# A two-layer cross-attention kernel on one core: the two layers as two phases, and MLP products from rounded halves

## What is computed

```python
# layer 0
h = ln(x, ln1);  q, k, v = h @ sa_wq, h @ sa_wk, h @ sa_wv
x = x + attn(rope(q * scale), rope(k), v, causal=True) @ sa_wo
h = ln(x, ln2);  q = h @ ca_wq;  k, v = y @ ca_wk, y @ ca_wv
x = x + attn(rope(q * scale), rope(k), v, causal=False) @ ca_wo
h = ln(x, ln3);  x = x + gelu_tanh(h @ fc1) @ fc2
# layer 1
q = x @ Wq.T;  k, v = y @ Wk.T, y @ Wv.T
x = x + attn(q * scale, k, v, causal=True)
x = ln(x);     out = x + gelu(x @ W1.T) @ W2.T
```

## Time and profile before

| | |
|---|---|
| median of 3 runs | 1119.66 us (1118.54 to 1122.07) |
| span of the profiled execution | 1118.3 us |
| own time of the profiled execution | not given beside its span; the span is 1.4 us under the median |
| PE busy | 936.4 us, 84% |
| DVE busy | 582.5 us, 52% |
| ACT busy | 419.9 us, 38% |
| POOL busy | 73.3 us, 7% |
| mean granted PE clock | 0.930 |

### The profile page before, as it was taken

The page is one execution under the profiler, slowest core; times in us unless marked ns, Lnnn a source line. Parts: engine busy times, 40 slices in busy tenths (PEclk is TensorE's granted clock), DMA queues, the critical chain, the costliest instruction groups (busy, mean ns, idle before and its releaser), DMA issues.

```text
span 1118.3 us, 13782 instructions
## 1 busy us (share of the span) xinstructions
PE 936.4 (84%) x5180; PEld 456.9 (41%) x5180; DVE 582.5 (52%) x1347; ACT 419.9 (38%) x822; POOL 73.3 (7%) x83
## 2 busy tenths in 40 slices
PE   3888864899988898888989867999887888987898
PEld 1433322345443353434445324633233454442365
DVE  5555637784667704488545675665125504415500
ACT  1133331342355625353422431167763323343421
POOL 2102000000000200000000001000000000000210
PEclk9988886799999999988999897999998999998999
DMA  7805462202132100645020401013004004022000
GB/s 275 102 1 73 75 139 43 24 2 27 23 38 30 29 1 20 94 51 66 1 30 1 57 13 17 10 40 48 1 20 57 2 1 57 2 37 22 1 19 19
DMA packets 47013, 43.85 MB, mean 39 GB/s; under 512 B 13510, under 2 KB 44386, under 8 KB 46434
## 3 DMA queue, kind: packets, MB, share of 16 engines
q1 hardware_dynamic: 46948, 42.98, 24.0%
HBM read 13.32 MB, written 2.10 MB: 14 GB/s over the span
## 4 chain that ended last, share of the span: by engine, by line
PE 57%; DVE 17%; DMA 10%; ACT 8%; SPq 5%; issue 4%; ACTq 0%; DVEq 0%
PE ps_exp L852 10%; PE ps_o L964 10%; PE ps_misc L835 10%; PE ps_max L889 8%; ACT probs L1200 5%; DVE mcol L1114 5%; SPq L695 4%; PE ps_exp L922 4%; DMA QA<-part 4%; PE ps_chain L814 3%; PE ps_chain L822 3%; DVE swap L1028 2%; DMA QC<-part 2%; PE ps_exp L927 2%; PE ps_chain L787 2%
## 5 line engine op out<-in xcount | busy, mean ns | idle before, releaser
L1114 DVE TENSOR_REDUCE mcol<-ps_max 128x3 f32<-128x462 f32 (+5 forms) x496 | 292.2, 626 | 181.9 <-PE ps_max L891 106.1
L1200 ACT ACTIVATE probs<-ps_exp 128x512 f32<-128x512 f32 (+3 forms) x544 | 261.1, 523 | 242.0 <-PE ps_exp L925 87.0
L889 PE MATMUL ps_max<-KA,QA 96*128 96x512 bf16 (+3 forms) x384 | 117.9, 359 | 55.3 <-DVE mcol L1114 24.4
L922 PE MATMUL ps_exp<-QA,KA 98*128 98x512 bf16 (+3 forms) x384 | 120.4, 350 | 26.1 <-ACT probs L1200 18.3
L835 PE MATMUL ps_misc<-hT,w_up 128*128 128x512 f32 x256 | 125.7, 615 | 7.2 <-ACT hid L1191 2.2
L852 PE MATMUL ps_exp<-w_down,hid 128*128 128x256 f32 x512 | 128.2, 388 | 0.0
L1191 ACT ACTIVATE hid<-ps_misc,col 128x512 f32<-128x512 f32 x64 | 44.0, 687 | 200.4 <-PE ps_misc L835 200.4
L852 PEld LDWEIGHTS ps_exp<-w_down,hid 128*128 128x128 f32 x512 | 94.5, 190 | 29.7 <-issue 15.5
L1248 POOL TENSOR_TENSOR part<-rot,part 128x512 bf16<-128x512 f32 (+1 forms) x36 | 40.8, 1133 | 923.2 <-DVE part L1038 923.2
L889 PEld LDWEIGHTS ps_max<-KA,QA 96*128 96x128 bf16 x384 | 39.2, 104 | 123.1 <-DVE mcol L1114 63.6
L964 PE MATMUL ps_o<-probs,V 128*17 128x512 f32 (+3 forms) x768 | 85.1, 517 | 3.2 <-ACT probs L1200 2.3
(11 more groups left out here) (109 smaller groups left out, 986.6 us busy)
## 6 DMA issues: line engine op xcount, KB each, us to landing
QA<-part SPq DMA_DIRECT2D x72, 128.0 KB, 5.1
QC<-part SPq DMA_DIRECT2D x72, 128.0 KB, 5.2
KA<-part SPq DMA_DIRECT2D x48, 128.0 KB, 5.2
xb<-in_x SPq DMA_DIRECT2D x8, 512.0 KB, 6.1
out<-xb SPq DMA_DIRECT2D x4, 512.0 KB, 3.0
KC<-part SPq DMA_DIRECT2D x24, 77.0 KB, 3.1
w_up<-in_fc SPq DMA_DIRECT2D x1, 1024.0 KB, 7.0
w_down<-in_fc SPq DMA_DIRECT2D x1, 1024.0 KB, 8.2
```

Of the source, the lines that this page charges most:

```text
L889: mm = pe.matmul(dst, q, kk, start=True, stop=not causal)
L922: mm = pe.matmul(bank[:, q0:CH], KA[:, g // NT, hh, (g % NT) * P:(g % NT + 1) * P], QA[:, hh, q0:CH], start=True, stop=(r < 0))
L1114: dve.tensor_reduce(dst, src, AX.X, ALU.max).then_inc(s_max_done, 1)
L1200: act.activation(probs[:, n % 2, h, q0:CH], ps_exp[exp_nth[s] % 2][:, q0:CH], ACT.Exp).then_inc(s_exp_done, 1)
```

## The change

1. **Two phases.** `post(c)` is cut into `layer0(c)` and `layer1(c)`. The thread of slot 0 now runs layer0 of chunks 0, 1 and 2 and then layer1 of chunks 2, 0 and 1. The x of chunks 0 and 1 goes to HBM after layer 0 (`save`) and comes back before layer 1 (`load3`), which waits until the chunk before it has been stored. A new step `phase2`, after the last `pv` of all self-attention, loads what layer 1 wants into the place of KA, V and the self-attention weights: w_up1, w_down1, KC1, l1_wq and the norm's rows. No step of layer 1 can come before it.
2. **MLP products.** Weights and activations are held as a high half (rounded to float32r) and a low half (the rest, also float32r). Each product is three float32r matmuls, high x high, high x low and low x high: `up` has 6 matmuls of 512 columns, `down` has 12 of 256. The input halves are made by two more ACT evictions and one POOL subtraction per `tr` of ln3 and ln4; the hidden halves by a second gelu on ACT and a POOL subtraction per `up`.
3. **Weights split at the start.** ACT loads the four weight matrices one by one to a staging place (`wload`), ACT rounds, POOL subtracts (`wsplit`), and layer 1's halves are written to HBM (`wsave`) ahead of layer 0's split. Layer 1's context keys go to HBM too (`keepkc`). `late` is gone.
4. **Context tail.** The four copies of the tail tokens are laid out as 128 columns in the input, so that one group of matmuls takes the place of four.
5. **Small moves.** `lnout` goes from POOL (8 operations) to DVE (2). The splitting of the bias rows goes from DVE to POOL, where it stands first. The planner's prices change with it.

```diff
-def post(c):
-    return (post_norm("sa", "ln2", c) + cross("ca", c) + out_norm("ca", "ln3", c)
-            + mlp(0, c) + [("tr", "x3", c, g) for g in range(NT // 2)] + cross("la", c)
+def layer0(c):
+
+    return post_norm("sa", "ln2", c) + cross("ca", c) + out_norm("ca", "ln3", c) + mlp(0, c)
+
+
+def layer1(c):
+
+    return ([("tr", "x3", c, g) for g in range(NT // 2)] + cross("la", c)
             + [("addatt", c, g) for g in range(NT // 2)] + norm("ln4", c) + [("lnout", c)] + mlp(1, c)
             + [("store", c)])
...
+KEPT = (0, 1)
+BEHIND = (2, 0, 1)
...
+def post():
+
+    out = []
+    for c in range(LAST):
+        out += layer0(c) + [("save", c)] * (c in KEPT)
+    for c in BEHIND:
+        out += [("load3", c)] * (c in KEPT) + layer1(c)
+    return out
...
+HALVES = ((0, 0), (0, 1), (1, 0))
...
                     for t in range(KT):
-                        mm = pe.matmul(bank[:, :], w_up[l][:, t, m * P:(m + 1) * P], hT_of("up", c)[:, t, :],
-                                       start=(t == 0), stop=(t == KT - 1))
+                        for i, j in HALVES:
+                            mm = pe.matmul(bank[:, :], w_up[l][:, i, t, m * P:(m + 1) * P], hup[:, j, t, :],
+                                           start=(t == 0 and (i, j) == HALVES[0]),
+                                           stop=(t == KT - 1 and (i, j) == HALVES[-1]))
...
-                        mm = pe.matmul(dst, hid[:, m % 2, t * P:(t + 1) * P], w_down[l][:, m, :],
-                                       start=False, stop=(m == NM - 1), skip_group_check=True)
+                        for i, j in HALVES:
+                            mm = pe.matmul(dst, hid[:, n % 2, i, t * P:(t + 1) * P], w_down[l][:, j, m, :],
+                                           start=False, stop=(m == NM - 1 and (i, j) == HALVES[-1]),
+                                           skip_group_check=True)
...
+                    gelu = (ACT.Gelu_apprx_tanh, ACT.Gelu)[l]
+                    act.activation(gel[:, n % 2, :], ps_misc[:, :], gelu, bias=c0(("fc1_b", "l1_b1")[l], m))
+                    act.activation(hid[:, n % 2, 0, :], ps_misc[:, :], gelu,
                                    bias=c0(("fc1_b", "l1_b1")[l], m)).then_inc(s_misc_free, 1)
...
+                elif k == "up":
+                    n = up_nth[s]
+                    after_misc(pool, s)
+                    pool.tensor_tensor(hid[:, n % 2, 1, :], gel[:, n % 2, :], hid[:, n % 2, 0, :],
+                                       ALU.subtract).then_inc(s_hid, 1)
...
+                if k == "wsplit":
+                    _, i, j = s
+                    src, high, _ = weight_half(i, j)
+                    if j == 0:
+                        act.wait_ge(s_stage[i % 2], 16 * (i // 2 + 1))
+                        if i > 1:
+                            act.wait_ge(s_wsaved[i % 2], 16)
+                    act.activation(high, src, ACT.Copy).then_inc(s_high, 1)
...
+                elif k == "wsave":
+                    i = s[1]
+                    act.wait_ge(s_wsplit, 2 * (i + 1))
...
-                    for j in range(HG):
-                        dst = bank[32 * j:32 * j + LYB, E:2 * E]
-                        add_bias(dst, name, LYB, start=False)
-                        for t in range(KT):
-                            mm = pe.matmul(dst, cT[:, t, b * LY + P:(b + 1) * LY], w_ctx[:, 2 * l + 1, t, :],
-                                           start=False, stop=(t == KT - 1), skip_group_check=True)
+                    dst = bank[:, E:2 * E]
+                    add_bias(dst, name, start=False)
+                    for t in range(KT):
+                        mm = pe.matmul(dst, cT[:, t, b, P:2 * P], w_ctxv[:, t, l, :],
+                                       start=False, stop=(t == KT - 1), skip_group_check=True)
```

More of the change, by code:

```diff
@@ L228, in order @@
     rings = {"max": [], "exp": [], "chain": [], "misc": [], "proj": [], "q": [], "c": []}
-    item = hidden = None
+    item = hidden = split = None
     def ring(s):
@@ L265, in before @@
                 w.append(("proj", "qs", c - 1, KT - 1))
+            if what == "oT_sa" and c == 0:
+                w.append(LAST_CTX)
         elif k == "proj":
@@ L283, in before @@
             w.append(("place", "qs", 0, 1))
+            if s[1] == 0:
+                w.append(("keepkc",))
+        elif k == "keepkc":
+            w += [("ctxk", 1, f) for f in range(KT)]
+        elif k == "wload" and s[1] > 1:
+            w.append(("wsplit", s[1] - 2, 1))
+        elif k == "wsplit":
+            w.append(("wload", s[1]))
+            if s[1] > 1:
+                w.append(("wsave", s[1] - 2))
+        elif k == "wsave":
+            w.append(("wsplit", s[1], 1))
+        elif k == "phase2":
+            w += [("pv", "sa", LAST, NHG - 1, groups("sa", LAST)[-1]), ("wsave", 1), ("keepkc",)]
         elif k == "ctxv":
@@ L326, in ready @@
         if hidden not in (None, i) and k in ("exp", "up"):
+            return None
+        if k == "tr" and s[1] in ("ln3", "ln4") and split not in (None, i):
             return None
@@ L394, in order @@
             gelu = k == "up"
+        if k == "tr" and s[1] in ("ln3", "ln4"):
+            free["act"] += 1.0
+            t = free["pool"] = max(free["pool"], t + 1.0) + 1.25
         if COST[k][-1][0] == "dma":
             t += DMA_LATENCY
+        t += LANDS.get(k, 0.0)
         fin[s] = t
@@ L1158, in _ @@
                                                  bias=c0(what + "_b", f), scale=c0(what + "_g", f))
+                    if what in ("ln3", "ln4"):
+                        if g == 0 and ups_done[s]:
+                            act.wait_ge(s_misc_ready, ups_done[s])
+                        for f in range(KT):
+                            ins = act.activation(hup[:, 0, f, 2 * g * P:(2 * g + 2) * P], src[:, f, :], ACT.Identity,
+                                                 bias=c0(what + "_b", f), scale=c0(what + "_g", f))
+                    elif what in NORMS:
+                        pass
                     else:
```

332 lines of the change are left out of this document (228 added, 104 removed).

## The result

The changed kernel takes 1204.45 us (1202.62 to 1207.7, 4 runs), the kernel before 1119.1 us on the same chip: a ratio of 1.0754, 95% interval 1.0711 to 1.0798. It is slower by some 84 us. The forecast was 1110 us, the range ended at 1160. Both the sign and the size are wrong.

The account below looks back on a forecast made before the run. PE looked like the bound, but outside a lone MLP it waits in turn for DVE, ACT and DMAs. Span 730 + 218 + 58 + 99 + 4 = 1109 us, 1110 us as a median; range 1065 to 1160.

Parts of the forecast that it names:

- the gain of the MLP: Three one-pass products save 4.3 us per MLP standing alone, 8 x 4.3 = 34 us in all.
- T1: Time up to the last self-attention product, the boundary between the phases: 824 us before, 730 us forecast (700 to 755).
- One pass for a float32r matmul, and loads 0.12 us apart: In the MLP on PE: 0.21 us per 512-column matmul, 1.3 us for `up`, 1.4 us for `down`.
- The rival with more passes: Float32r matmuls or their loads in the MLP cost more than assumed: 1171 us, 1251 us if `up` pays too; 8%.
- The pace of 2.9 us: MLP step time, set by ACT: `up` m+1 waits in ps_misc for both gelus of m; 2.9 us in place of 3.44.
- MLP = 8 x 2.9 + 3 = 26 us: Price of each whole MLP in phase 2: eight steps of 2.9 us plus 3 us.
- A head group takes 5.57 us: Cross-attention head group with no maxima to wait for: 5.57 us, 22 us for four.
- part one: First part of phase 2, layer 0 and 1 of chunk 3 and layer 1 of chunk 2: 218 us (205 to 235).
- Chunk 1 alone: Chunk 1's layer 1 at the end with nothing beside it: 99 us, plus 4 us for the falling clock.
- Lost cover: Slower rival: phase 1's exponentials and the end lack other work to fill waits, clock at 0.70: 1147 us; 22%.
- The late subtraction: Slower rival: POOL's subtraction slows beside DVE's two-SBUF-operand work, MLP pace about 3.3 us: +26, 1136 us; 7%.
- The change does not do what it says: Rival: MLP pace stays 3.44 us from two gelus and two waits, 34 us less gain: 1144 us; within 22%.

Follow-up runs that it names:

- two_phase_f32: The changed kernel with the plain float32 MLP of before, phases, context tail and small moves kept: 1204.8 us, 1.0783 of the kernel before.
- phases_no_low: The changed kernel with the high part in place of the MLP's input and hidden low parts, same product count, one gelu: 1161.8 us, 1.0381 of the kernel before.
- phases_fill: The changed kernel with idle bf16 matmuls in PE's waits in layer 1 of chunks 0 and 1: 1199.7 us, 1.0754 of the kernel before.
- phases_pair: The changed kernel with layer 1 of chunk 1 in chunk 3's buffers and thread, beside layer 1 of chunk 0: 1186.6 us, 1.0603 of the kernel before.
- phases_pair_late: phases_pair with chunk 0's last MLP made to wait until chunk 1's last attention product is placed: 1167.4 us, 1.0399 of the kernel before.
- halves_in_place: The kernel before, not phased, replanned for shorter MLP steps, with MLP products as three bf16 products, low halves subtracted in place: 1124.2 us, 1.0044 of the kernel before.
- experiment 4: The same run as halves_in_place: the kernel before with MLP products as three bf16 products, low halves subtracted in place: 1124.2 us, 1.0044 of the kernel before.
- ctx_only: The kernel before with only the context tail from one group of products, one planner price changed: 1113.6 us, 0.9954 of the kernel before.
- halves_same_order: halves_in_place in exactly the order of the kernel before, weight splits placed behind the context's keys and the first MLP: 1102.4 us, 0.9843 of the kernel before.

## Why the prediction was wrong, step by step

The experiments split the 94 us between the forecast and the measurement in two. The forecast gave the MLPs 34 us of gain, so for the phases alone its own terms give 1110 + 34 = 1144 us, a cost of 25 us; two_phase_f32 measured 85. And the 34 us themselves were not there. So **two steps failed: the gain of the MLP (34 us forecast, nothing measured) and the price of the phases (25 us forecast, 85 measured)**, and the second is the larger. The terms, one by one:

- **T1 = 730 us: right**, 739.2 us measured. Two of its terms were seen more or less alone: the context tail, -7 predicted, -5 (-2 to -8) measured; the start, +3 predicted: the first self-attention product starts 8 us later (83.5, against 75.9 in the earlier trace rows). The three MLPs were to give 13; two_phase_f32, with float32 MLPs and a slightly other order, reached T1 at 745.0, 6 us later. That layer 1 of chunks 0 and 1 frees about its own PE time is borne out by equal idle time before T1. The other terms were not seen alone, so the sum may owe some of its fit to luck. One small slip stands in it: the parts of a half chunk's PE work add up to 52 us, not 53.
- **One pass for a float32r matmul, and loads 0.12 us apart: right.** Where nothing waits (phases_no_low), six take 1144.97 - 1143.59 = 1.38 us and twelve 1146.35 - 1144.97 = 1.38, against 1.3 and 1.4. The rival with more passes is out.
- **The pace of 2.9 us: right mechanism, mis-sized.** ps_misc and the two gelus do set it, but it is 3.13. The gelus' 1.26 us (1181.65 to 1182.91) and the 0.15 back are as forecast; from `up`'s start to the first gelu it is 1181.65 - 1179.93 = 1.72 us, not 1.5. A step saves 0.31 us, not 0.54.
- **"MLP = 8 x 2.9 + 3 = 26 us": the term that failed most.** Measured from the first `up` to the first addition, it took 34.3, 35.9, 36.0, 35.3 and 32.8 us for the five behind T1, some 44 us more than 5 x 26. The "+3" left out the slow first `up`s, a table load and four bias products on PE: 32.8 - 8 x 3.13 = 7.8 us, not 3. In the first three, work of other chunks on PE stands in between as well. The kernel before had a good part of this: by the same marks its four MLPs behind T1 took 32.6, 32.9, 33.7 and 29.6 us, 2 to 6 us more than eight steps of 3.44, and I had read only the steady rows. The 29.6 are those of the last one (1083.69 to 1113.31), which follows the MLP ahead of it without a wait:

```profile
1083.69 1.88 PE L835 MATMUL ps_misc<-hT,w_up 128*128 128x512 f32 x4
...
1113.31 0.69 DVE L1054 TENSOR_TENSOR xb<-xb,ps_exp 128x512 f32<-128x512 f32 x1 [28.74 <-PE ps_exp L852]
```

So the last MLP is 3 us longer than before, not 4.3 shorter. At its like place in two_phase_f32 the float32 MLP takes 33.2 us: three products save about 0.3 us there, and the split ahead of them takes 3. For the whole kernel two_phase_f32 shows the sum, nothing.
- **"A head group takes 5.57 us", 22 for four: true where the rows were read, too short elsewhere.** Chunk 3's four take 34 us (first exponentials 787, last eviction 821), since maxima of its own and of chunk 2 stand among them on PE; layer 1's take 30 us from the addition before (23 predicted). The norms took 15 and 21 us, not 13 and 15. With three of the MLPs (28 us more) this makes most of part one's 282 us in place of 218. Chunk 0's end took 72 us in place of 58, 9 of them in its MLP.
- **Chunk 1 alone, "99" and 4 for the clock: 110 us** (1093.4 to 1203.4). Its MLP, 32.8 us for 26, is as large as the 7 missing. The clock's 4 were 7 by phases_fill; some of these lie in the MLP's first two `up`, so the two do not simply add.
- **Lost cover (1147 us): the right rival, mis-sized and misplaced.** It priced phase 1 and the clock; phase 1 lost nothing, and the clock 7 us in the lone chunk. The price lies behind T1, in a rule that the forecast named and did not price: "The exponentials and the MLPs exclude each other" was used only to add up a chain. It also means that the exponentials of the other side cannot enter the gaps of a chunk in its MLP. phases_pair and phases_pair_late, which only arrange the last two chunks otherwise, took back 33 to 40 us. What the rest of the phases' 85 us consists of was not shown one by one.
- **The late subtraction: it exists at the MLP's head, not in its pace.** Beside DVE's `lnout` the subtractions took this:

```profile
891.72 1.22 DVE L1199 TENSOR_TENSOR xb<-a_ctx,g4b 128x1024 f32<-128x1024 f32 x1
891.88 2.07 POOL L1441 TENSOR_TENSOR part<-rot,part 128x512 bf16<-128x512 f32 x1 [12.72 <-DVE part L1177]
892.97 2.06 DVE L1200 TENSOR_TENSOR xb<-xb,g4b 128x1024 f32<-128x1024 f32 x1
893.91 3.47 POOL L1458 TENSOR_TENSOR hup<-hT,hup 128x512 fp32r<-128x512 f32 x2
```

One took 2.07 us in place of 1.15 and the two of `hup` 3.47 in place of 2.52, so chunk 2's first `up` waited about 2 us more. This agrees with the Trainium skill (SBUF — State Buffer, Who interferes with whom), which states that a DVE instruction with two SBUF inputs contends with a GpSimd instruction that reads SBUF. The change itself had moved `lnout` to DVE, to just this place; the forecast called it free. The same shows the other way round in halves_in_place (experiment 4), where DVE lost 4.8 us in four products. In the steady MLP no such instruction is there, and POOL's 1.28 us lie beside the next `up`.
- **"The change does not do what it says", 1144 us**: true of the MLP (no net gain), for the reason given there (two gelus and two waits) and for one not given, the split ahead of the first `up`.

What stays open: the phases' cost beyond the 40 us, how much of it is the clock between 740 and 1021 us, and why the gains of ctx_only and halves_same_order do not add up. Float32r in the old order was not tried: its halves take twice the room of the weights, which the old order does not have in SBUF.

## What to carry to other kernels

Before work is put off to a later phase, list what will stand beside it: at the end of a span idle time counts in full, and PE's busy share behind the boundary (86% before, 73% after) is the number to forecast, not its work. Price a block by one measured whole, head and tail with it, since eight steps of a steady pace left out a quarter of it. And a cheaper product is worth what is left after its operands are made: three one-pass products gained 18 us where the halves cost one POOL instruction beside other work, and nothing where they cost a second gelu in the bank's turn and a split with four more evictions ahead. Last, two executions of the same order of steps were 13 us apart at 1072 us, so a gain is best read behind the point where two orders part.

## What the runs showed that I had not expected

- The upper half of a float32 word serves as a bf16 operand in place: six matmuls of 512 columns with both operands at every second element take 1081.52 - 1080.17 = 1.35 us, next to 1.38 for six of float32r.
- A weight load of bf16 for `down` took 99 ns on the page's average, one of float32r 195 ns; yet twelve products took much the same, 2.71 - 1.35 = 1.36 us and 1.38 us. So the longer load cost the products nothing here.
- In these kernels the granted clock in lone stretches (0.76) cost only some 7 us of 110, with PE busy for 67 of 106 us.
- While POOL read and wrote SBUF for 7.8 us, four small DVE products of two SBUF operands took 6.09 us in place of 1.29.
- Putting one MLP 14 us later made a kernel 2% faster, 12 us of it by the trace where the orders differ.
